# An interaction tower (DLRM): layer blocks moved between gram and lookups, and the copies shared out anew

## The chip, the cores and the metric

One core of one Trainium2 chip. The metric is the device time of one launch in microseconds, the median of several runs. Times inside a run are from the profile, in us from the start of its span.

## The reference

2048 samples, 27 features. Each feature is a row of 128 floats from a table of its own (1000 to 125000 rows). All pairs of the 27 rows of a sample are multiplied (351 products), and three layers follow.

```python
e = jnp.stack([tbl_0[ids[:, 0]], ..., tbl_26[ids[:, 26]]], axis=1)
x = einsum('bfd,bgd->bfg', e, e)[pairs with g < f]
z = concatenate([bottom, x], axis=1)
h = concatenate([z, bottom], axis=1)
h = maximum(h @ W_top1 + b_top1, 0.0)
h = maximum(h @ W_top2 + b_top2, 0.0)
y = h @ W_top3
```

W_top1 is 607x512, W_top2 512x256, W_top3 256x1. All is fp32.

## The kernel before

The samples go through in 16 halves of 128 (`HALF`). Two halves make a tile of 256, and the layers work on units (`u`): seven whole tiles and the last tile in two units of 128.

Features come in two ways. 17 tables are **gathered**: GpSimd (POOL) issues one indirect DMA for each table and half (L311), into `rows`, a ring of two halves; five groups of 4, 4, 3, 3 and 3 tables. TensorE turns each group (`transpose`, L705, three or four transposes into a column bank) and ScalarE or VectorE copies it into `eT`. Ten small tables are **looked up** (hot tables): VectorE compares ids with row numbers to make 0/1 masks (`make_masks`, L582 and L586), and TensorE multiplies table parts by the masks (`look_up`, L686). One lookup serves a window of four halves, so each half has one or two lookups (32 or 52 matmul records x2) for later halves. Their results are copied from the column banks to `eH` (L424 on ScalarE, L599 on VectorE) and placed in `eT` by ScalarE (`place_hot`, L438). There are three column banks, used in the order of the list `FILLS`; `on_scalar` tells which engine copies a fill.

`multiply_pairs` (the gram, L722) multiplies the features of each sample with each other; ScalarE and VectorE copy the result into `pairs` (`copy_pairs`, L468 and L617), and SyncE moves it into `x` in nine DMAs (`load_x`). The last half's nine are shared by SyncE, ScalarE and GpSimd.

The layers: `layer1(u, blocks)` has four blocks m = 0 to 3, each of 4 matmuls (one with `bottom` at L741, three with `x` at L745; fp32 matmuls show as two records each, so a block has 8). `layer2` (L777) has 8 matmuls, `layer3` (L787) 8 small ones. Blocks 0 and 1 and layer 2 write `mlp_bank[0]`, blocks 2 and 3 and layer 3 `mlp_bank[1]`. ScalarE does `relu1` (L477), `relu2` (L484) and `copy_y` (L493). For the last unit `last_layer1_bottom` (L756) and `last_layer1_pairs` (L766) use the free column and gram banks.

Each engine runs its own list written out by hand; semaphores tie them together. TensorE's for a half h, before:

```python
for g in groups_of(h): transpose(h, g)
if h % 2 == 0:
    layer3(h // 2 - 2); layer1(h // 2 - 1, range(2))
elif h >= 3: layer2(h // 2 - 1)
multiply_pairs(h)
for n in AFTER[h]: look_up(n)
if h % 2 == 0: layer1(h // 2 - 1, range(2, 4))
```

GpSimd's list has only the gathers, each group waiting until the group two halves earlier is transposed, then the last three DMAs of x.

Of the kernel before, what the change touches and what calls it, by code (L numbers as in the profile page):

```python
# [133 lines left out]
def on_scalar(fill):  # L134

    return fill < FRONT_FILLS or fill % 2 == 1
# [9 lines left out]
def build(nc, tables, idx_d, hot_ids_d, bottom_d, w1_d, wa_d, wb_d, b1_d, w2_d, b2_d, w3_d, ident_d, rowid_d, out_d):  # L146
# [6 lines left out]
    with ctx:  # L153
# [133 lines left out]
        def layer3_out(u):  # L287
            _, _, size = unit_columns(u)
            if u == TILES:
                return gram_bank[0].rearrange("p q g -> p (q g)")[:, 0:size // Y_STRIPS]  # L290
            return mlp_bank[1][:, 0, 0:size // Y_STRIPS]
# [41 lines left out]
        def _(sp):  # L333
# [62 lines left out]
            for h in range(HALVES):  # L396
                if h % 2 == 0:
                    load_bottom(h // 2)
                    if h >= 4:
                        store_y(h // 2 - 2)  # L400
# [4 lines left out]
            store_y(TILES - 2)  # L405
            store_y(TILES - 1)
# [4 lines left out]
        def _(act):  # L411
# [59 lines left out]
            def relu1(u, b):  # L471
                _, at, size = unit_columns(u)
                act.wait_ge(l1_full, 2 * u + b + 1)
# [51 lines left out]
            for h in range(1, HALVES):  # L525
                for g in groups_of(h):
                    copy_transposed(h, g)
                if h % 2 == 0 and h >= 4:
                    copy_y(h // 2 - 2)
                copy_pairs(h)  # L530
                if h % 2 == 0:
                    relu1(h // 2 - 1, 0)
                elif h >= 3:
                    relu2(h // 2 - 1)
# [9 lines left out]
            for r in range(1, len(BLOCKS), 3):  # L544
                out, src = x_block(LAST, r)
                nc.scalar.dma_start(out, src).then_inc(x_loaded[LAST % 2], 16)
            copy_y(TILES - 2)
            relu1(TILES - 1, 0)
            relu1(TILES - 1, 1)
# [10 lines left out]
        def _(dve):  # L560
# [30 lines left out]
            def copy_lookup(n):  # L591
                for k in LOOKUPS[n][0]:
                    fill = lookup_fill(n, k)
                    if not on_scalar(fill):

                        dve.wait_ge(col_full[fill % BANKS], fill // BANKS + 1)
                        dve.wait_ge(hot_copied, LOOKUPS[n][1])
                        out, src = looked_up(n, k)
                        nc.vector.tensor_copy(out, src).then_inc(col_copied[fill % BANKS], 1)  # L599

# [36 lines left out]
            def masks_behind_gram(h):  # L637

                n = AFTER[h][0]
                pair_used = entries_to(n + 1) + MASKS  # L640
                make_entries(entries_to(n) + MASKS, pair_used)
                copy_lookup(n)
                for single in AFTER[h][1:]:
                    make_entries(pair_used, entries_to(single + 1) + MASKS)
                    copy_lookup(single)
# [18 lines left out]
        def _(pe):  # L664
# [63 lines left out]
            def layer1(u, blocks):  # L728
                buf, at, size = unit_columns(u)
                for m in blocks:  # L730
                    if m == 0:
# [4 lines left out]
                        if u > 0:  # L736
                            pe.wait_ge(h2_made, u)
# [147 lines left out]
```

## Time and profile before

| what | value |
|---|---|
| median of 3 runs | 411.26 us (410.33 to 411.98) |
| the profiled execution | 408.87 us, span 406.9 us |
| TensorE matmul busy | 355.6 us, 87% |
| GpSimd busy | 293.9 us, 72% |
| VectorE busy | 231.5 us, 57% |
| ScalarE busy | 156.5 us, 38% |
| mean granted clock of TensorE | 0.966 of full |

The span runs from the first to the last instruction; the execution's own time is 2 us longer. Busy time of GpSimd counts the gather instructions alone, the 0.30 us between them are not in it.

### The profile page before, as it was taken

To read this page: it belongs to the slowest core of one execution; us is meant where nothing else is said; L and a number is where in the kernel's file an instruction comes from. 1 tells how busy PE (TensorE), PEld (TensorE's weight loads), DVE (VectorE), ACT (ScalarE), POOL (GpSimd) and SP (SyncE) were. 2 spreads that over 40 slices of the span, in tenths; PEclk is the share of its full clock that TensorE was granted. 3 is DMA by queue.
4 is the path that set the end of the run, shared out by engine and by line. 5 is a ranking of instruction groups with operands and counts; after the bars stand their busy time and mean duration, and the time that the engine had idled before them with its cause. 6 is when DMAs were issued, how large, how long until landed. Compare 5 with 4: busy or idle time off the path is not lost.

```text
span 406.9 us, 9147 instructions
## 1 busy us (share of the span) xinstructions
PE 355.6 (87%) x3669; PEld 305.4 (75%) x3669; DVE 231.5 (57%) x430; ACT 156.5 (38%) x337; POOL 293.9 (72%) x284
## 2 busy tenths in 40 slices
PE   0679888979997999989996999989997899869986
PEld 0678667858885888868885788868885798749876
DVE  1588985857747274858746173856746163816120
ACT  2245624225343244325352243425244153505342
POOL 5777887777777787777777777777778777777210
PEclk9999996999999899999999799999999899969999
DMA  7968952323414131323324222322513222322100
GB/s 194 249 183 218 269 149 69 116 78 82 149 53 129 55 86 57 117 72 109 126 58 124 54 73 67 115 79 78 144 53 100 57 74 65 85 72 68 32 21 2
DMA packets 20737, 40.50 MB, mean 100 GB/s; under 512 B 7128, under 2 KB 11428, under 8 KB 20696
## 3 DMA queue, kind: packets, MB, share of 16 engines
q1 hardware_dynamic: 11674, 21.64, 18.6%
q0 software_dynamic: 8960, 18.22, 16.5%
q8 instruction: 29, 0.48, 0.5%
q14 instruction: 12, 0.10, 0.1%
q10 hardware_dynamic: 62, 0.06, 0.1%
HBM read 36.81 MB, written 0.01 MB: 90 GB/s over the span
## 4 chain that ended last, share of the span: by engine, by line
PE 48%; POOL 33%; issue 11%; DMA 4%; DVE 2%; DVEq 1%; ACT 0%; ACTq 0%
POOL rows L311 31%; PE col_bank L686 17%; PE gram_bank L722 9%; PE mlp_bank L745 9%; PE col_bank L705 4%; PE mlp_bank L777 4%; DMA rows<-in_tbl,idx 4%; PE mlp_bank L741 3%; POOL h L322 1%; DVEq L589 1%; PE mlp_bank L787 1%; DVE mask L582 1%; DVE mask L586 1%; DMA idx<-in_gather_ids 1%; PE gram_bank L777 1%
## 5 line engine op out<-in xcount | busy, mean ns | idle before, releaser
L311 POOL DMA_INDIRECT rows<-in_tbl,idx x272 | 286.4, 1053 | 85.4 <-issue 79.5
L686 PE MATMUL col_bank<-mask,parts 125*128 125x512 f32 (+3 forms) x768 | 163.7, 374 | 16.5 <-DVE mask L582 16.5
L686 PEld LDWEIGHTS col_bank<-mask,parts 125*128 125x128 f32 x768 | 135.8, 198 | 39.0 <-DVE parts L623 15.6
L582 DVE TENSOR_SCALAR mask<-hot_i,rowid 125x1024 fp32r<-125x1024 int32 (+3 forms) x152 | 103.4, 681 | 20.0 <-PE col_bank L686 9.8
L617 DVE COPY pairs<-gram_bank 26x208 f32<-26x208 f32 x128 | 46.7, 365 | 79.4 <-PE gram_bank L722 58.0
L468 ACT ACTIVATE pairs<-gram_bank 26x208 f32<-26x208 f32 x128 | 44.3, 346 | 80.1 <-PE gram_bank L722 60.4
L705 PE MATMUL col_bank<-ident,rows 128*128 128x128 f32 x272 | 41.3, 290 | 27.4 <-DMA rows<-in_tbl,idx 14.3
L722 PEld LDWEIGHTS gram_bank<-eT 128*58 128x58 f32 x2048 | 56.9, 135 | 7.9 <-issue 7.6
L722 PE MATMUL gram_bank<-eT 128*58 128x52 f32 x2048 | 59.0, 218 | 2.4 <-ACT eT L438 1.6
L705 PEld LDWEIGHTS col_bank<-ident,rows 128*128 128x128 f32 x272 | 31.8, 147 | 36.2 <-DMA rows<-in_tbl,idx 17.1
L438 ACT ACTIVATE eT<-eH 128x256 f32<-128x256 f32 (+1 forms) x64 | 43.4, 790 | 17.8 <-DVE eH L599 16.9
L424 ACT ACTIVATE eH<-col_bank 128x512 f32<-128x512 f32 (+3 forms) x30 | 15.2, 516 | 87.5 <-PE col_bank L686 77.1
L745 PE MATMUL mlp_bank<-x,w 126*128 126x256 f32 (+3 forms) x192 | 48.4, 391 | 0.0
L607 DVE COPY eT<-col_bank 128x384 f32<-128x384 f32 (+2 forms) x42 | 25.3, 611 | 38.3 <-PE col_bank L705 37.5
L745 PEld LDWEIGHTS mlp_bank<-x,w 126*128 126x128 f32 (+1 forms) x192 | 38.1, 207 | 6.2
L586 DVE TENSOR_SCALAR mask<-hot_i,rowid 125x512 fp32r<-125x512 int32 (+2 forms) x80 | 33.6, 467 | 5.0 <-PE col_bank L686 1.9
L432 ACT ACTIVATE eT<-col_bank 128x384 f32<-128x384 f32 (+2 forms) x41 | 21.7, 553 | 19.4 <-PE col_bank L705 19.2
L777 PE MATMUL mlp_bank<-h,w 128*128 128x256 f32 (+1 forms) x128 | 27.4, 367 | 0.0
L777 PEld LDWEIGHTS mlp_bank<-h,w 128*128 128x128 f32 x128 | 22.6, 190 | 2.5
L741 PE MATMUL mlp_bank<-bottom,w 128*128 128x256 f32 (+1 forms) x64 | 21.2, 416 | 0.0
L623 DVE TENSOR_TENSOR parts<-pairs,parts 125x1024 fp32r<-125x1024 f32 (+1 forms) x10 | 12.6, 1281 | 12.1 <-ACT parts L415 6.1
L477 ACT ACTIVATE h<-mlp_bank,b 128x256 f32<-128x256 f32 (+1 forms) x32 | 13.0, 457 | 13.5 <-PE mlp_bank L745 13.2
(34 smaller groups left out, 75.6 us busy)
## 6 DMA issues: line engine op xcount, KB each, us to landing
hot_i<-in_hot_ids SPq DMA_DIRECT2D x13, 512.0 KB, 4.0
rows<-in_tbl,idx POOLq DMA_INDIRECT x272, 3.0
pairs<-in_tbl SPq DMA_DIRECT2D x8, 448.0 KB
hot_i<-in_hot_ids SPq DMA_DIRECT2D x8, 256.0 KB, 3.3
pairs<-in_tbl SPq DMA_DIRECT2D x2, 560.0 KB
bottom<-in_bottom SPq DMA_DIRECT2D x8, 128.0 KB, 4.0
hot_i<-in_hot_ids SPq DMA_DIRECT2D x2, 384.0 KB, 4.6
x<-pairs SPq DMA_DIRECT2D x16, 39.0 KB
```

What stands on the lines that cost most here:

```text
L311: pool.indirect_dma_start(out=rows_of(h, g)[:, i * D:(i + 1) * D], out_offset=None, in_=tables[GATHERED_TABLES[f]], in_offset=bass.Indirec ...
L438: return nc.scalar.activation(eT[:, :, first:last].rearrange("p s f -> p f s"), eH[:, first:last, at:at + HALF], ACT.Copy)
L468: last = nc.scalar.activation(pairs_of(s, 1, j), gram_of(n % BANKS, 1, j), ACT.Copy)
L582: last = nc.vector.tensor_scalar(mask[0:ROWS, entry % MASKS, 0:2 * size], ids, row_of(ks[0], c), None, ALU.is_equal)
L586: last = nc.vector.tensor_scalar(mask[0:ROWS, entry % MASKS, i * size:(i + 1) * size], ids, row_of(ks[0], 2 * c + i), None, ALU.is_equal)
L617: last = nc.vector.tensor_copy(pairs_of(s, 0, j), gram_of(n % BANKS, 0, j))
L686: last = nc.tensor.matmul(col_bank[fill % BANKS][:, 0:size], parts[k][0:ROWS, part, c * D:(c + 1) * D], mask[0:ROWS, entry % MASKS, at:at ...
L705: last = nc.tensor.transpose(col_bank[fill % BANKS][:, i * HALF:(i + 1) * HALF], src, ident[:, :])
L722: last = nc.tensor.matmul(gram_bank[n % BANKS][COLUMNS * t:COLUMNS * t + GRAM_ROWS, q, 0:PACK * (F - 1)], eT[:, a:a + PACK, :].rearrange(" ...
L741: nc.tensor.matmul(layer1_out(u, m), w1[:, X_CHUNKS, m * 128:(m + 1) * 128], bottom[:, buf, at:at + size], start=True, stop=False)
L745: last = nc.tensor.matmul(layer1_out(u, m).rearrange("p (h s) -> p h s", s=HALF), w1[0:k, c, m * 128:(m + 1) * 128], x[0:k, buf, at // HAL ...
L777: last = nc.tensor.matmul(layer2_out(u, m), w2[:, c, m * 128:(m + 1) * 128], h1[:, c, at:at + size], start=(c == 0), stop=(c == N1 // 128 ...
```

## The change

- `on_scalar`: ScalarE copies every lookup; of the five groups of transposes in a half it copies 1 and 3 (from half 1 on), VectorE 0, 2 and 4 (and the extra group 5 goes to ScalarE). Before, odd fills went to ScalarE and even ones to VectorE, whatever they were.
- VectorE: `copy_lookup` is gone, and `masks_behind_gram` makes the same masks in the same order in one go.
- TensorE: layer 1's blocks run in the order 2, 3, 0, 1. Block 2 stands ahead of an even half's gram, blocks 3 and 0 behind its lookups, block 1 ahead of the odd half's gram, and layer 2 behind that half's lookups. Layer 3 moves from the even half to the odd one behind it.
- The tail: behind the last transposes stand layer 3 of unit 5, block 1 of unit 6, the gram, layer 2 of unit 6, the bottom matmuls of the last unit, layer 1 of unit 7, layer 3 of unit 6 (now in a gram bank), layer 2 of unit 7; from there it is as before.
- ScalarE and SyncE follow: `relu2` in even halves, `copy_y` and `relu1(u, 0)` in odd ones ahead of `copy_pairs`; the store of y one even half later; in the tail ScalarE issues its three DMAs of x ahead of `relu2` of unit 6.

TensorE's rows around the last two halves' transposes, before: from the transposes of half 14 (L705, from `rows` into `col_bank`) over layer 3 (L787) and layer 1 (L741, L745) to the gram (L722), the lookups (L686), two blocks and the transposes of half 15.

```order
L705 MATMUL col_bank<-ident,rows 128x128 x17
L787 MATMUL mlp_bank<-h,w 32x64 x8
L741 MATMUL mlp_bank<-bottom,w 128x256
L745 MATMUL mlp_bank<-x,w 128x256 x3
L741 MATMUL mlp_bank<-bottom,w 128x256
L745 MATMUL mlp_bank<-x,w 128x256 x3
L722 MATMUL gram_bank<-eT 58x52 x64
L686 MATMUL col_bank<-mask,parts 128x128 x52
L741 MATMUL mlp_bank<-bottom,w 128x256
...
L705 MATMUL col_bank<-ident,rows 128x128 x17
```

The same place in the changed kernel (its lines are L692 for transposes, L728 and L732 for layer 1, L709 for the gram, L673 for lookups, L781 for layer 3):

```order
L692 MATMUL col_bank<-ident,rows 128x128 x17
L728 MATMUL mlp_bank<-bottom,w 128x256
L732 MATMUL mlp_bank<-x,w 128x256 x3
L709 MATMUL gram_bank<-eT 58x52 x64
L673 MATMUL col_bank<-mask,parts 128x128 x52
L728 MATMUL mlp_bank<-bottom,w 128x256
...
L692 MATMUL col_bank<-ident,rows 128x128 x17
L781 MATMUL mlp_bank<-h,w 32x64 x8
L728 MATMUL mlp_bank<-bottom,w 128x256
L732 MATMUL mlp_bank<-x,w 128x256 x3
L709 MATMUL gram_bank<-eT 58x52 x64
```

One block and layer 3 have moved from between the two halves' transposes to behind the last ones. What stood behind the last transposes before, up to layer 2 of unit 7:

```order
L777 MATMUL mlp_bank<-h,w 128x256 x8
L722 MATMUL gram_bank<-eT 58x52 x64
L787 MATMUL mlp_bank<-h,w 32x64 x8
L741 MATMUL mlp_bank<-bottom,w 128x128
...
L756 MATMUL col_bank<-bottom,w 128x128 x3
L756 MATMUL gram_bank<-bottom,w 128x128
L777 MATMUL mlp_bank<-h,w 128x128 x8
```

And now, from layer 2 of unit 6 on (L765 is layer 2, L744 the bottom matmuls):

```order
L765 MATMUL mlp_bank<-h,w 128x256 x8
L744 MATMUL col_bank<-bottom,w 128x128 x3
L744 MATMUL gram_bank<-bottom,w 128x128
L728 MATMUL mlp_bank<-bottom,w 128x128
...
L781 MATMUL gram_bank<-h,w 32x64 x8
L765 MATMUL mlp_bank<-h,w 128x128 x8
```

Layer 2 of unit 6 stands behind the gram instead of ahead of it, and the bottom matmuls ahead of layer 1 of unit 7 instead of behind it.

```diff
--- before.py
+++ after.py
@@ -133,7 +133,8 @@
 
 def on_scalar(fill):
 
-    return fill < FRONT_FILLS or fill % 2 == 1
+    what = FILLS[fill]
+    return fill < FRONT_FILLS or what[0] == "lookup" or what[2] % 2 == 1
 
 
 def unit_columns(u):
@@ -286,8 +287,9 @@
 
         def layer3_out(u):
             _, _, size = unit_columns(u)
-            if u == TILES:
-                return gram_bank[0].rearrange("p q g -> p (q g)")[:, 0:size // Y_STRIPS]
+            if u in (TILES - 2, TILES):
+                first = 0 if u < TILES else TILE // Y_STRIPS
+                return gram_bank[0].rearrange("p q g -> p (q g)")[:, first:first + size // Y_STRIPS]
             return mlp_bank[1][:, 0, 0:size // Y_STRIPS]
 
         block = ctx.enter_context(nc.Block())
@@ -396,14 +398,14 @@
             for h in range(HALVES):
                 if h % 2 == 0:
                     load_bottom(h // 2)
-                    if h >= 4:
-                        store_y(h // 2 - 2)
+                    if h >= 6:
+                        store_y(h // 2 - 3)
                 load_x(h, range(0, len(BLOCKS), 3) if h == LAST else range(len(BLOCKS)))
                 if h + 1 < LAST:
                     for n in AFTER[h + 1][1:] + (AFTER[h + 2][:1] if h + 2 < LAST else []):
                         load_hot_ids(n)
-            store_y(TILES - 2)
-            store_y(TILES - 1)
+            for t in range(TILES - 3, TILES):
+                store_y(t)
 
             sp.wait_ge(y_stored, 16 * TILES)
 
@@ -470,7 +472,7 @@
 
             def relu1(u, b):
                 _, at, size = unit_columns(u)
-                act.wait_ge(l1_full, 2 * u + b + 1)
+                act.wait_ge(l1_full, 2 * u + (1 if b == 1 else 2))
                 if u == 0 and b == 0:
                     act.wait_ge(w1_summed, 1)
                 for m in range(2 * b, 2 * b + 2):
@@ -526,12 +528,12 @@
                 for g in groups_of(h):
                     copy_transposed(h, g)
                 if h % 2 == 0 and h >= 4:
-                    copy_y(h // 2 - 2)
+                    relu2(h // 2 - 2)
+                elif h >= 3:
+                    if h >= 5:
+                        copy_y(h // 2 - 2)
+                    relu1(h // 2 - 1, 0)
                 copy_pairs(h)
-                if h % 2 == 0:
-                    relu1(h // 2 - 1, 0)
-                elif h >= 3:
-                    relu2(h // 2 - 1)
                 if h < LAST:
                     place_early(h + 1)
                     for n in AFTER[h]:
@@ -544,9 +546,10 @@
             for r in range(1, len(BLOCKS), 3):
                 out, src = x_block(LAST, r)
                 nc.scalar.dma_start(out, src).then_inc(x_loaded[LAST % 2], 16)
+            relu2(TILES - 2)
+            relu1(TILES - 1, 1)
+            relu1(TILES - 1, 0)
             copy_y(TILES - 2)
-            relu1(TILES - 1, 0)
-            relu1(TILES - 1, 1)
             relu2(TILES - 1)
             for m in range(N1 // 128):
                 act.wait_ge(l1_full, 2 * TILES + m + 1)
@@ -588,16 +591,6 @@
                     last.then_inc(masks_made, 1)
                     dve.drain()
 
-            def copy_lookup(n):
-                for k in LOOKUPS[n][0]:
-                    fill = lookup_fill(n, k)
-                    if not on_scalar(fill):
-
-                        dve.wait_ge(col_full[fill % BANKS], fill // BANKS + 1)
-                        dve.wait_ge(hot_copied, LOOKUPS[n][1])
-                        out, src = looked_up(n, k)
-                        nc.vector.tensor_copy(out, src).then_inc(col_copied[fill % BANKS], 1)
-
             def copy_transposed(h, g):
                 fill = transpose_fill(h, g)
                 if not on_scalar(fill):
@@ -636,13 +629,7 @@
 
             def masks_behind_gram(h):
 
-                n = AFTER[h][0]
-                pair_used = entries_to(n + 1) + MASKS
-                make_entries(entries_to(n) + MASKS, pair_used)
-                copy_lookup(n)
-                for single in AFTER[h][1:]:
-                    make_entries(pair_used, entries_to(single + 1) + MASKS)
-                    copy_lookup(single)
+                make_entries(entries_to(AFTER[h][0]) + MASKS, entries_to(AFTER[h][-1] + 1) + MASKS)
 
             for k in LATE:
                 make_low(k)
@@ -728,16 +715,16 @@
             def layer1(u, blocks):
                 buf, at, size = unit_columns(u)
                 for m in blocks:
-                    if m == 0:
+                    if m == 2:
 
                         for half in ((0, 1) if u < TILES - 1 else (0,)):
                             pe.wait_ge(x_loaded[half], 16 * len(BLOCKS) * (u + 1))
                         pe.wait_ge(bottom_loaded[buf], 16 * (u // 2 + 1))
-                        if u > 0:
-                            pe.wait_ge(h2_made, u)
-                    if m == 2 and u > 0:
-
-                        pe.wait_ge(y_made, u)
+                        if u > 1:
+                            pe.wait_ge(y_made, u - 1)
+                    if m == 0 and u > 0:
+
+                        pe.wait_ge(h2_made, u)
                     nc.tensor.matmul(layer1_out(u, m), w1[:, X_CHUNKS, m * 128:(m + 1) * 128], bottom[:, buf, at:at + size],
                                      start=True, stop=False)
                     for c in range(X_CHUNKS):
@@ -752,6 +739,7 @@
             def last_layer1_bottom():
 
                 pe.wait_ge(gram_copied[1], STRIPS * used(HALVES * SETS, 1))
+                pe.wait_ge(bottom_loaded[(TILES - 1) % 2], 16 * ((TILES - 1) // 2 + 1))
                 for m in range(N1 // 128):
                     nc.tensor.matmul(layer1_out(TILES, m), w1[:, X_CHUNKS, m * 128:(m + 1) * 128],
                                      bottom[:, (TILES - 1) % 2, HALF:TILE], start=True, stop=False)
@@ -781,6 +769,12 @@
             def layer3(u):
                 _, at, size = unit_columns(u)
                 pe.wait_ge(h2_made, u + 1)
+                if u < TILES - 2:
+
+                    pe.wait_ge(h1_made, 2 * (u + 1) + 1)
+                elif u == TILES - 2:
+
+                    pe.wait_ge(gram_copied[0], STRIPS * used(HALVES * SETS, 0))
                 part = size // Y_STRIPS
                 for c in range(N2 // 128):
                     for t in range(Y_STRIPS):
@@ -804,26 +798,30 @@
                 for g in groups_of(h):
                     transpose(h, g)
                 if h % 2 == 0:
-                    if h >= 4:
-                        layer3(h // 2 - 2)
                     if h == 2:
                         pe.wait_ge(weights_loaded, 16 * WEIGHT_LOADS)
                         pe.wait_ge(w1_summed, 1)
-                    layer1(h // 2 - 1, range(2))
+                    layer1(h // 2 - 1, (2,))
                 elif h >= 3:
-                    layer2(h // 2 - 1)
+                    if h >= 5:
+                        layer3(h // 2 - 2)
+                    layer1(h // 2 - 1, (1,))
                 multiply_pairs(h)
                 for n in AFTER[h]:
                     look_up(n)
                 if h % 2 == 0:
-                    layer1(h // 2 - 1, range(2, 4))
+                    layer1(h // 2 - 1, (3, 0))
+                elif h >= 3:
+                    layer2(h // 2 - 1)
             for g in range(NG):
                 transpose(LAST, g)
+            layer3(TILES - 3)
+            layer1(TILES - 2, (1,))
+            multiply_pairs(LAST)
             layer2(TILES - 2)
-            multiply_pairs(LAST)
+            last_layer1_bottom()
+            layer1(TILES - 1, (2, 3, 0, 1))
             layer3(TILES - 2)
-            layer1(TILES - 1, range(4))
-            last_layer1_bottom()
             layer2(TILES - 1)
             last_layer1_pairs()
             layer2(TILES)
```

## Rows read from the trace of the kernel before

**Rows 1.** Page, busy us (share of the span) x instructions.
```profile
PE 355.6 (87%) x3669; PEld 305.4 (75%) x3669; DVE 231.5 (57%) x430; ACT 156.5 (38%) x337; POOL 293.9 (72%) x284
```

**Rows 2.** Page, groups: count | busy us, mean ns | idle before, releaser.
```profile
L311 POOL DMA_INDIRECT rows<-in_tbl,idx x272 | 286.4, 1053 | 85.4 <-issue 79.5
```

**Rows 3.** Waits of POOL: us in total, times, longest us.
```profile
POOL rows L311 <- PE col_bank L705: 1.8, 6, 0.3
```

**Rows 4.** Timeline of POOL, its last gather: start us, us, instruction.
```profile
378.58 0.94 POOL L311 DMA_INDIRECT rows<-in_tbl,idx  x1 [0.30 <-issue]
```

**Rows 5.** Waits of PE, the two largest behind the start.
```profile
PE col_bank L705 <- DMA rows<-in_tbl,idx: 14.3, 10, 3.6
PE col_bank L705 <- DVE eH L599: 7.4, 5, 3.1
```

**Rows 6.** Timeline of PE, 300 to 407 us.
```profile
356.21 0.52 PE L705 MATMUL col_bank<-ident,rows 128*128 128x128 f32 x3 [1.47 <-DMA rows<-in_tbl,idx]
360.29 0.90 PE L705 MATMUL col_bank<-ident,rows 128*128 128x128 f32 x3 [3.56 <-DMA rows<-in_tbl,idx]
...
361.71 1.22 PE L741 MATMUL mlp_bank<-bottom,w 128*128 128x256 f32 x2
362.72 2.75 PE L745 MATMUL mlp_bank<-x,w 124*128 124x256 f32 x6
...
376.54 0.65 PE L741 MATMUL mlp_bank<-bottom,w 128*128 128x256 f32 x2
...
380.06 2.35 PE L705 MATMUL col_bank<-ident,rows 128*128 128x128 f32 x17
382.25 3.62 PE L777 MATMUL mlp_bank<-h,w 128*128 128x256 f32 x16
385.80 3.62 PE L722 MATMUL gram_bank<-eT 128*58 128x52 f32 x128
391.07 0.43 PE L787 MATMUL mlp_bank<-h,w 128*32 128x64 f32 x16 [1.65 <-ACT h L484]
391.43 0.49 PE L741 MATMUL mlp_bank<-bottom,w 128*128 128x128 f32 x2
...
395.35 0.83 PE L756 MATMUL col_bank<-bottom,w 128*128 128x128 f32 x6
...
396.24 2.04 PE L777 MATMUL mlp_bank<-h,w 128*128 128x128 f32 x16
```

**Rows 7.** Chain that ended last; then the gathers' tile, 350 to 385.
```profile
357.35 2.90 DMA rows<-in_tbl,idx
...
DMA to landing us min/median/max: 2.4/2.6/3.5
```

**Rows 8.** Timeline of all engines, 194.9 to 196.5 us.
```profile
195.01 0.94 POOL L311 DMA_INDIRECT rows<-in_tbl,idx  x1 [0.30 <-issue]
195.12 0.69 DVE L599 COPY eH<-col_bank 128x512 f32<-128x512 f32 x1 [0.16 <-issue]
...
196.26 1.18 POOL L311 DMA_INDIRECT rows<-in_tbl,idx  x1 [0.30 <-issue]
```

**Rows 9.** Windows: PE, PEld, DVE, ACT, POOL busy, PEclk, DMA, GB/s.
```profile
128.00:220.00 92.00, 85.92 (x880) 72.29 (x878) 55.17 (x102) 35.54 (x78) 71.58 (x68) 0.98 0.30 90
220.00:311.00 91.00, 85.74 (x869) 71.85 (x870) 52.16 (x97) 35.08 (x77) 70.58 (x68) 0.96 0.30 87
```

**Rows 10.** Timeline of all engines, 376 to 407 us.
```profile
391.47 1.61 ACTq L546 DMA_DIRECT2D x<-pairs  x2
...
395.55 0.62 ACT L477 ACTIVATE h<-mlp_bank,b 128x128 f32<-128x128 f32 x2 [1.40 <-PE mlp_bank L745]
```

**Rows 11.** Timeline of PE, 0 to 200 us.
```profile
62.36 3.01 PE L705 MATMUL col_bank<-ident,rows 128*128 128x128 f32 x13 [3.13 <-DVE eH L599]
...
177.57 0.84 PE L705 MATMUL col_bank<-ident,rows 128*128 128x128 f32 x6 [1.80 <-DVE eT L607]
```

**Rows 12.** Windows of PE: us, busy (count), PEclk, DMA share, GB/s.
```profile
364.00:365.00 1.00, 1.00 (x4) 0.50 0.19 62
```

## The prediction

> **What bounds the kernel now.** I read the busy shares first, then GpSimd's stream, then what TensorE waits for, and last the end of the run in order of time. TensorE is busy 87% of the span [rows 1], which looks like the bound. It isn't the one that sets the pace. GpSimd's group of gathers shows 272 gathers of 1.053 us each and 85.4 us idle, 79.5 of it only issue [rows 2]: 0.30 us ahead of each gather, as the two of [rows 8] show. Its longest wait put down to TensorE is also 0.3 us [rows 3], so it never waited for a transpose to free a buffer. It starts its last gather at 378.58 and ends it at 379.52 [rows 4]. TensorE on the other hand waits for landed rows 10 times, 14.3 us in all [rows 5]. The worst is at half 14: it transposes three tables at 356.21, then stands 3.56 us until the last group has landed and goes on at 360.29 [rows 6]; the chain shows that transfer as the releaser, 2.90 us after its issue [rows 7]. So up to half 14 the gathers set the time, and TensorE catches up with them again and again. From 360.29 it has 19.8 us of work up to the last half's transposes at 380.06 [rows 6], and the last gathers land just then. In this one stretch TensorE and GpSimd are level; everything behind 382.25 is a tail of TensorE alone.
>
> **The change part by part.** The sum is made on the profiled execution, 408.87 us with a span of 406.9; the median of the runs shown is 411.26, 2.4 more, and I add my difference to that.
>
> *Layer 1 and 2 in the halves.* No matmul is added or removed. A unit's work was 4 blocks of layer 1 and the 2 blocks of layer 2, and an even half carried all four layer 1 blocks, one of 1.76 us (two take 376.54 to 380.06 [rows 6]), an odd half layer 2, 3.55 us (382.25 to 385.80). Now an even half has three layer 1 blocks and an odd one layer 3 (0.36, 391.07 to 391.43), the fourth block and layer 2. TensorE comes 2.1 us later to the transposes of even halves, where it waits for rows anyway, and 2.1 us sooner to those of odd halves, the last half's among them, since block m=1 and layer 3 are no longer ahead of them. What it finds there is rows that haven't landed. Price in the halves: 0, covered by GpSimd's stream, which doesn't wait for TensorE; if that cover were gone, these microseconds would be a gain.
>
> *Two blocks between lookups and transposes.* Before, the transposes of an even half came right behind the lookups and waited for copies out of the column banks: 7.4 us in 5 waits for VectorE's lookup copies [rows 5]. These go, with 3.5 us of layer work in front of them. Late next are the landed rows; so 0 again.
>
> *Who copies.* VectorE gives up its 16 lookup copies and ScalarE takes them, one or so in each half, at about the 0.69 us that VectorE needs [rows 8]. ScalarE then places the hot columns, then copies its two groups of transposes. Its queue grows by 0.7 us a half, where 3.5 us of matmuls now give it room. In half 2 there is no layer work behind half 1's lookups; a stall of a microsecond is possible there, and the wait for rows at half 4 covers it. VectorE copies three of five groups in every half. For GpSimd the question is whether its gathers get quicker. They take 0.94 us in quiet and more beside masks: 1.18 at 196.26 beside the mask instructions. Beside a lookup copy (195.12, 0.69 us) the gather of 195.01 takes 0.94 [rows 8]. All masks stay, so their price of 272 x (1.053 - 0.94) = 31 us stays. It could drift with the phase of masks against gathers: two stretches of four halves with the same masks have 71.58 and 70.58 us of GpSimd for 68 gathers [rows 9]. From this I take 0 and, over the whole run, 1 us either way. The bounds without this argument are the full 31 us below, excluded since no mask is dropped, and a like amount above, excluded since no mask is added.
>
> *SyncE.* The store of y moves one even half later, and the loads of x stay in place; a store stands behind nothing that TensorE waits for until the tail, where the y of unit 6 is needed only for the last layer 3 copy, some 6 us later. 0.
>
> *The tail.* The last transposes can't start before the last three gathers have landed. The last one is issued at 378.58; landing took 2.4 to 3.5 us, median 2.6, in this stretch [rows 7]. With 2.6 they land at 381.2, and three transposes take 0.5 (356.21), which gives 381.7 against the 382.25 of before (there the copy of a bank was also late): -0.55, between -0.75 and +0.4.
> Behind them stood before: layer 2 3.55, gram 3.62 with a wait of 1.65 for ScalarE's h2, layer 3 0.36, layer 1 of unit 7 3.92 (391.43 to 395.35), the bottom blocks 0.89, and layer 2 of unit 7 at 396.24: 13.99 us [rows 6].
> Now stand there: layer 3 of unit 5 0.36, layer 1's block m=1 1.76, gram 3.6, layer 2 3.55, bottom 0.89, layer 1 of unit 7 3.92, and then a wait. The bottom blocks used to cover ScalarE's relu (395.55, 0.62 us [rows 10]); now only layer 3's 0.36 lies there, so from the end of layer 1 to layer 2 it stays 0.89. Sum 14.97, that is +0.98. The wait of 1.65 is gone, and in its place stand the block of 1.76 and layer 3's 0.36 that came in from half 14, and the bare relu.
> The relu of layer 2 of unit 6 is now queued on ScalarE behind its three transfers of x, two of which took 1.61 us [rows 10]; with gram ending 3 to 4 us before layer 2 does, it runs near the end of layer 2, and layer 1 needs it only after two blocks and the bottom (about 2.8 us). 0. Everything behind 396.24 is unchanged.
> Total: -0.55 + 0.98 = +0.4 us. The forecast is 411.7, its own range 410.4 to 413.1 (1 us of GpSimd's drift and the bounds of the landing).
>
> **The rivals.** Within 0.5%, 2.06 us, a measurement of this kernel can't tell from no change.
>
> *B, slower: TensorE's clock is low in the tail.* TensorE now waits longer in one piece. A wait of 1.80 us at 177 left the matmuls at full speed; one of 3.13 us ahead of 62.36 was followed by 13 transposes in 3.01 us [rows 11], against 0.52 for three (356.21). After the waits of 356 to 360 the granted clock was 0.50, 1.2 GHz, still in 364 to 365 [rows 12], and a block took from 361.71 to 365.47, 3.7 us, against 1.8. Whether this happens at the last transposes hangs on half 14. If the clock is low there as before, TensorE comes to the last transposes 1.76 and some 0.5 sooner than 380.06, near 377.8, needs 1.8 for the first 14 and waits 1.6 us until 381.2: no fall. If half 14 runs at full speed, it is there 2.2 sooner, near 375.6, and waits over 3 us: a fall. In half 14 TensorE was free at 354.74 (356.21 less the wait of 1.47 [rows 6]); 2.1 later and with three more transposes that is 357.3, a wait of 3.0 before 360.29, at the edge as well. So it could go either way. The price is transposes 0.4 and the block 1.9, 2.2 with rounding: 411.7 + 2.2 = 413.9. It decides once the wait before the last three transposes is beyond about 3 us.
> The Trainium skill (TensorE: Matmul & The Clock Gate, section "Why this matters for your kernels") warns against idle gaps between bursts, since the array goes back to half rate. It speaks against this change, which puts TensorE's waits together; by that rule alone B would be the forecast. The trace agrees for 3.13 us and not for 1.80.
>
> *A, faster: gathers gain from VectorE's missing copies.* If a lookup copy cost GpSimd what a mask does, 1.18 - 0.94 = 0.24 us, 16 fewer would give 4 us: 407.7. Against it stands the gather of 0.94 beside the copy [rows 8].
> The Trainium skill (SBUF — State Buffer, section "Who interferes with whom") counts copies among VectorE's operations that can take the port pair shared with GpSimd. Measured by its word alone A would hold; the row here speaks against it for a copy out of PSUM.
>
> *C, faster: TensorE is the bound after all.* Then the vanished stalls count: 7.4 us for lookup copies, and with them 411.3 - 7.4 = 403.9. It needs GpSimd to be waiting somewhere, and [rows 2, 3] show no such place.
>
> **How the numbers follow.** The forecast has 54%: 3 of them over 0.5% faster, 5 slower by the drift, 46 in between. B has 32%: 27 slower, 5 still within 0.5%, since 413.3 is the border. A has 10%, C 4%, both faster. That makes faster 0.17, same 0.51, slower 0.32. The range takes in the forecast and B with their bounds, from 409.4 to 414.4, and leaves A and C out.
>
> **What would show it.** In the changed profile GpSimd's gathers still run without a pause and end near 379.5; TensorE's waits for lookup copies are nearly gone and its waits for landed rows are up from 14.3 to over 20 us; the last transposes end near 381.7; layer 2 of unit 7 starts near 396.7, at full clock. If it starts near 399 with a granted clock of 0.50 behind the last transposes, B is right. If the last gather ends before 377, A is. If gathers show pauses above 0.3 us, my bound is wrong.

## The result, and the profile after

The changed kernel takes 413.15 us, the median of 15 runs (411.8 to 414.15); the kernel before took 410.82 us beside it (15 runs, 408.74 to 412.85). The ratio is 1.0047 with a 95% interval of 1.003 to 1.0064: slower by 1.9 us, 0.5%, at the very border of what counts as no change here. The interval reaches from 1.2 to 2.6 us, and the two medians as they stand are 2.3 us apart. The change's profiled execution took 413.02 us with a span of 411.2, near its median. The profiled execution of before, at 408.87, was 2 us below its own. So the two spans, 411.2 and 406.9, lie 4.3 us apart, of which about half belongs to these two samples and not to the change.

From the page of the changed kernel, first the busy times, then GpSimd's group:

```profile
PE 356.6 (87%) x3669; PEld 305.4 (74%) x3669; DVE 223.9 (54%) x417; ACT 162.9 (40%) x350; POOL 296.7 (72%) x284
...
L313 POOL DMA_INDIRECT rows<-in_tbl,idx x272 | 287.9, 1059 | 85.3 <-issue 79.9
```

As before [rows 1, 2]: TensorE 87% busy, and GpSimd's 272 gathers at 1.059 us, with 79.9 of the 85.3 us ahead of them only issue and no wait for TensorE above 0.3 us. TensorE's waits in the changed kernel (us in total, times, longest us):

```profile
PE col_bank L692 <- DMA rows<-in_tbl,idx: 25.9, 14, 3.3
...
PE col_bank L692 <- DVE eT L600: 3.8, 2, 2.9
...
PE mlp_bank L765 <- ACT h L479: 0.4, 1, 0.4
```

The 7.4 us for lookup copies [rows 5] are gone. The waits for landed rows have grown from 14.3 to 25.9 us. That is most of the story of the halves: what TensorE no longer waits for copies, it waits for rows.

The tail in TensorE's timeline (start us, us, instruction, idle before and its releaser); it answers to [rows 6], from the last half's transposes to layer 2 of unit 7:

```profile
379.00 2.00 PE L692 MATMUL col_bank<-ident,rows 128*128 128x128 f32 x14
383.81 0.85 PE L692 MATMUL col_bank<-ident,rows 128*128 128x128 f32 x3 [2.82 <-DMA rows<-in_tbl,idx]
384.59 0.65 PE L781 MATMUL mlp_bank<-h,w 128*32 128x64 f32 x16
385.17 1.22 PE L728 MATMUL mlp_bank<-bottom,w 128*128 128x256 f32 x2
386.18 2.03 PE L732 MATMUL mlp_bank<-x,w 124*128 124x256 f32 x6
388.14 3.62 PE L709 MATMUL gram_bank<-eT 128*58 128x52 f32 x128
...
400.59 2.05 PE L765 MATMUL mlp_bank<-h,w 128*128 128x128 f32 x16 [0.35 <-ACT h L479]
```

and the granted clock behind the wait (us, busy, clock, DMA share, GB/s):

```profile
384.00:385.00 1.00, 1.00 (x19) 0.50 0.00 0
...
386.00:387.00 1.00, 1.00 (x3) 0.50 0.00 0
387.00:388.00 1.00, 1.00 (x5) 0.84 0.00 0
```

TensorE is done with 14 of 17 transposes at 381.0, stands 2.82 us, and comes back at 0.50 of the clock, 1.2 GHz. Layer 3 then takes 0.58 instead of 0.36 and the block 2.97 from 385.17 to 388.14, where half 14's own block at full clock takes 1.83 (364.24 to 366.07). That is rival B of the prediction. From the start of the last gather to layer 2 of unit 7 it is 19.36 us (381.23 to 400.59) against 17.66 before (378.58 to 396.24): the tail has 1.7 of the 4.3 us between the spans.

### The profile page after: what moved, and what is told of

It reads as the page before. It is cut to its first block, busy times and chain, and to the rows that moved or that the text cites. A ratio compares the mean times of both kernels' runs of the same rounds, so it can differ in the third digit from the quotient of the medians.

```text
span 411.2 us, 9138 instructions
## 1 busy us (share of the span) xinstructions
PE 356.6 (87%) x3669; PEld 305.4 (74%) x3669; DVE 223.9 (54%) x417; ACT 162.9 (40%) x350; POOL 296.7 (72%) x284
## 4 chain that ended last, share of the span: by engine, by line
POOL 37%; PE 32%; issue 13%; DMA 9%; DVE 5%; DVEq 2%; ACT 1%; SPq 1%; POOLq 0%
POOL rows L313 37%; PE col_bank L673 11%; PE gram_bank L709 7%; PE mlp_bank L732 4%; DVE mask L585 4%; DMA rows<-in_tbl,idx 4%; PE mlp_bank L765 3%; DMA hot_i<-in_hot_ids 3%; PE col_bank L692 2%; DVEq L592 2%; PE mlp_bank L728 2%; DMA pairs<-in_tbl 2%; DMA h<-in_tbl,idx 1%; PE gram_bank L765 1%; ACT parts L417 0%
## 5 line engine op out<-in xcount | busy, mean ns | idle before, releaser
L313 POOL DMA_INDIRECT rows<-in_tbl,idx x272 | 287.9, 1059 | 85.3 <-issue 79.9
L673 PE MATMUL col_bank<-mask,parts 125*128 125x512 f32 (+3 forms) x768 | 162.8, 372 | 17.3 <-DVE mask L585 17.3
L673 PEld LDWEIGHTS col_bank<-mask,parts 125*128 125x128 f32 x768 | 134.8, 197 | 39.9 <-DVE parts L616 15.7
L600 DVE COPY eT<-col_bank 128x384 f32<-128x384 f32 (+1 forms) x45 | 27.5, 616 | 76.4 <-PE col_bank L692 75.3
L692 PE MATMUL col_bank<-ident,rows 128*128 128x128 f32 x272 | 40.4, 286 | 30.8 <-DMA rows<-in_tbl,idx 25.9
L709 PEld LDWEIGHTS gram_bank<-eT 128*58 128x58 f32 x2048 | 58.3, 137 | 9.4 <-issue 9.4
L709 PE MATMUL gram_bank<-eT 128*58 128x52 f32 x2048 | 60.3, 221 | 2.7 <-ACT eT L440 2.1
L426 ACT ACTIVATE eH<-col_bank 128x512 f32<-128x512 f32 (+3 forms) x46 | 22.5, 530 | 96.1 <-PE col_bank L673 95.9
L692 PEld LDWEIGHTS col_bank<-ident,rows 128*128 128x128 f32 x272 | 31.2, 144 | 39.2 <-DMA rows<-in_tbl,idx 30.1
L732 PE MATMUL mlp_bank<-x,w 126*128 126x256 f32 (+3 forms) x192 | 50.0, 400 | 0.0
L732 PEld LDWEIGHTS mlp_bank<-x,w 126*128 126x128 f32 (+1 forms) x192 | 38.9, 211 | 6.4
L434 ACT ACTIVATE eT<-col_bank 128x384 f32<-128x384 f32 (+3 forms) x38 | 20.2, 545 | 43.3 <-PE col_bank L692 43.3
L765 PE MATMUL mlp_bank<-h,w 128*128 128x256 f32 (+1 forms) x128 | 27.5, 367 | 0.4 <-ACT h L479 0.4
L765 PEld LDWEIGHTS mlp_bank<-h,w 128*128 128x128 f32 x128 | 22.9, 190 | 3.5 <-ACT h L479 0.5
L728 PE MATMUL mlp_bank<-bottom,w 128*128 128x256 f32 (+1 forms) x64 | 21.3, 417 | 0.0
```

The lines of the kernel that those rows point to most:

```text
L313: pool.indirect_dma_start(out=rows_of(h, g)[:, i * D:(i + 1) * D], out_offset=None, in_=tables[GATHERED_TABLES[f]], in_offset=bass.Indirec ...
L673: last = nc.tensor.matmul(col_bank[fill % BANKS][:, 0:size], parts[k][0:ROWS, part, c * D:(c + 1) * D], mask[0:ROWS, entry % MASKS, at:at ...
L692: last = nc.tensor.transpose(col_bank[fill % BANKS][:, i * HALF:(i + 1) * HALF], src, ident[:, :])
L709: last = nc.tensor.matmul(gram_bank[n % BANKS][COLUMNS * t:COLUMNS * t + GRAM_ROWS, q, 0:PACK * (F - 1)], eT[:, a:a + PACK, :].rearrange(" ...
L728: nc.tensor.matmul(layer1_out(u, m), w1[:, X_CHUNKS, m * 128:(m + 1) * 128], bottom[:, buf, at:at + size], start=True, stop=False)
L732: last = nc.tensor.matmul(layer1_out(u, m).rearrange("p (h s) -> p h s", s=HALF), w1[0:k, c, m * 128:(m + 1) * 128], x[0:k, buf, at // HAL ...
```

## Where the rest of the span's difference came from

GpSimd's last gather starts later than in [rows 4]:

```profile
381.23 0.95 POOL L313 DMA_INDIRECT rows<-in_tbl,idx  x1 [0.30 <-issue]
```

That is 2.65 us behind 378.58. Its timeline in the changed kernel at the start, with its 21st and its 34th gather last:

```profile
10.99 1.89 POOL L313 DMA_INDIRECT rows<-in_tbl,idx  x1 [0.30 <-issue]
...
20.96 1.92 POOL L313 DMA_INDIRECT rows<-in_tbl,idx  x1 [0.30 <-issue]
...
28.19 1.96 POOL L324 DMA_INDIRECT h<-in_tbl,idx  x1 [0.31 <-issue]
...
31.71 1.13 POOL L313 DMA_INDIRECT rows<-in_tbl,idx  x1 [0.30 <-issue]
...
51.00 0.95 POOL L313 DMA_INDIRECT rows<-in_tbl,idx  x1 [0.30 <-issue]
```

and in the kernel before, the same two last:

```profile
7.22 1.95 POOL L311 DMA_INDIRECT rows<-in_tbl,idx  x1 [0.30 <-issue]
...
28.20 1.97 POOL L311 DMA_INDIRECT rows<-in_tbl,idx  x1 [0.30 <-issue]
30.47 0.96 POOL L311 DMA_INDIRECT rows<-in_tbl,idx  x1 [0.30 <-issue]
...
49.78 0.94 POOL L311 DMA_INDIRECT rows<-in_tbl,idx  x1 [0.31 <-issue]
```

Single gathers take 1.9 us in the first 30 us of both, three of them in one trace and two in the other. By the 21st gather the changed kernel is 1.24 us behind (31.71 against 30.47), by the 34th 1.22. The rest comes later: from the 34th gather to the last it is 328.80 us before and 330.23 after, 1.4 us more, most of it from gathers beside masks, which take 1.0 to 1.6 us. So about half of the 2.65 us is from the start and half is drift. Whether that drift comes of the moved copies or would show between two traces of one kernel, a single full trace of before can't say.

## The experiments

The theory after the result: the change is slower because its tail starts with a long wait and then runs at half the clock. The rival: GpSimd's gathers end later because masks and copies now meet them differently. All kernels with a label ending in b or c are repeats, since on three of the chips used every kernel, the one before too, took over 530 us. What those chips did is told further down.

**One block in the wait (e5b).** The changed kernel with one block of layer 1 computed twice.

```diff
-            for g in range(NG):
+            for g in range(NG - 1):
                 transpose(LAST, g)
+            layer1(TILES - 2, (0,))
+            transpose(LAST, NG - 1)
             layer3(TILES - 3)
             layer1(TILES - 2, (1,))
```

> Once more on another chip, since on the first one every kernel took over 530 us. The changed kernel with one block of layer 1 (unit 6, m=0, the same values once more) computed a second time ahead of the last group of transposes. Clock theory: the wait there shrinks from about 3 us to 1.3, the clock stays at its full level, and the time falls by 2.2 us to about 0.4 above before, although TensorE does more. Rival (gathers end later since the copies moved): 2 us slower than before.

Measured: 410.8 us (12 runs) against 410.65 of before, ratio 1.0006 (0.9989 to 1.0023). TensorE computes 4 more matmuls and the time is 1.7 us less than the change's (1.0047 less 1.0006, of 411). The two weren't measured side by side but each against before; from the two intervals I estimate the 1.7 as good to 1 us either way. Its timeline of TensorE, then the last gather, then the clock:

```profile
377.62 2.00 PE L692 MATMUL col_bank<-ident,rows 128*128 128x128 f32 x14
379.46 0.60 PE L728 MATMUL mlp_bank<-bottom,w 128*128 128x256 f32 x2
...
382.53 0.55 PE L692 MATMUL col_bank<-ident,rows 128*128 128x128 f32 x3 [1.18 <-DMA rows<-in_tbl,idx]
383.01 0.43 PE L781 MATMUL mlp_bank<-h,w 128*32 128x64 f32 x16
383.37 0.70 PE L728 MATMUL mlp_bank<-bottom,w 128*128 128x256 f32 x2
...
385.30 3.62 PE L709 MATMUL gram_bank<-eT 128*58 128x52 f32 x128
...
397.75 2.05 PE L765 MATMUL mlp_bank<-h,w 128*128 128x128 f32 x16 [0.35 <-ACT h L479]
```

```profile
379.80 0.94 POOL L313 DMA_INDIRECT rows<-in_tbl,idx  x1 [0.30 <-issue]
```

```profile
383.00:384.00 1.00, 1.00 (x20) 1.00 0.00 0
```

The wait is 1.18 us instead of 2.82, and the clock stays at 1.00. From the last transposes to layer 2 of unit 7 it is 15.22 us (382.53 to 397.75) against 16.78 in the change (383.81 to 400.59): 1.56 us, which is the 1.7 of the medians. The work between the two points is the same. The clock theory holds. The late gathers can't explain this: they end 1.4 us earlier in this one trace, but with that taken out, from the last gather to layer 2 of unit 7, it is still 17.95 us (379.80 to 397.75) against 19.36, and medians of 12 and 15 runs hang little on one trace's gathers.

**Only the copies (e1b).** The kernel before with the new `on_scalar`, VectorE's `copy_lookup` taken out and its masks made in one go.

```diff
-    return fill < FRONT_FILLS or fill % 2 == 1
+    what = FILLS[fill]
+    return fill < FRONT_FILLS or what[0] == "lookup" or what[2] % 2 == 1
...
```

> Once more on another chip. The kernel before with the copies alone changed. Clock theory: no difference, within 0.5 us of before, since the tail is that of before. Rival (gathers): about 2 us slower than before, and the last gather starts near 381 instead of 378.6.

Measured: 411.76 us against 410.65, ratio 1.0025 (1.0002 to 1.0047), between the two expectations. GpSimd's timeline, the 34th gather and the last, and TensorE's tail:

```profile
51.06 0.94 POOL L312 DMA_INDIRECT rows<-in_tbl,idx  x1 [0.30 <-issue]
...
381.14 0.94 POOL L312 DMA_INDIRECT rows<-in_tbl,idx  x1 [0.30 <-issue]
```

```profile
384.11 3.62 PE L762 MATMUL mlp_bank<-h,w 128*128 128x256 f32 x16
...
398.14 2.04 PE L762 MATMUL mlp_bank<-h,w 128*128 128x128 f32 x16
```

The last gather is as late as in the change, at 381.14: 1.28 us behind before by the 34th gather, and another 1.28 from there to the last (330.08 us against 328.80). The tail from layer 2 of unit 6 to that of unit 7 is 14.03 us against 13.99 in [rows 6], so the copies cost nothing there. In e5b, which has the same copies, the stretch from the 34th gather to the last is 329.20 us, 0.4 more than before, and the time is level with before, at most 0.9 us above it by its interval. So the three traces with moved copies drift by 0.4, 1.3 and 1.4 us against the one of before. What the copies have in that, and in the 1.0 us of this run, whose interval reaches down to 0.1 us, is left open.

**Fewer gathers (f1, f2).** Both kernels without the gathers of the last two tables from half 2 on, 28 of 277; their products are made of stale rows.

```diff
                         f = first + i
+                        if h >= 2 and f >= GATHERED - 2:
+                            continue
```

> The kernel before without the gathers of the last two tables from half 2 on: 28 of 277 are left out, and stale rows stand in their place in the products. If GpSimd's stream paces the kernel, 28 x 1.36 = 38 us less of it moves the bound to TensorE: the time falls by about the waits for rows (14 us) and the time at half clock behind them (some 6), to about 391, and no further. If TensorE is the bound already, it stays within 2 us of before.

> The changed kernel without the same 28 gathers. Pace theory: here the waits for copies that the change removed count at last, so it is faster than the kernel before with fewer gathers by 5 to 9 us, about 384. Rival (the change gains nothing on TensorE either): equal to or slower than the other by the 2 us that it loses now.

Measured: before with fewer gathers 387.81 us (ratio 0.9421 to before, 0.9351 to 0.9492), the change with fewer 375.77 (0.915, 0.9098 to 0.9202). The bound was GpSimd's stream: without a tenth of it both get faster. And the change, worth -1.9 us as it stands, is worth 12.0 us by the medians of 4 runs each (11 by the two ratios) once GpSimd is out of the way, where I expected 5 to 9. The kernel before fell further than the 391 that I expected too: TensorE's busy time went down from 355.6 to 345.7 us at the same number of matmuls, its mean granted clock up from 0.966 to 0.990. In the changed kernel it went from 356.6 to 344.3 us and from 0.963 to 0.995. From these busy times I estimate that the matmuls at half clock cost TensorE 10 to 12 us in the full kernels, not some 6. TensorE's waits in the kernel before with fewer gathers, and the one that GpSimd now has for TensorE:

```profile
PE col_bank L707 <- DVE eH L601: 7.5, 5, 3.1
PE col_bank L707 <- DVE eT L609: 5.0, 3, 1.8
PE col_bank L707 <- ACT eT L434: 2.8, 4, 0.9
...
PE mlp_bank L789 <- ACT h L486: 1.7, 1, 1.7
```

```profile
POOL rows L313 <- PE gram_bank L724: 7.6, 3, 4.0
```

and in the changed one:

```profile
PE col_bank L694 <- DVE eT L602: 3.7, 2, 2.9
...
PE col_bank L694 <- DMA rows<-in_tbl,idx: 1.6, 3, 0.6
```

These four are 17.0 us of waits for copies (7.5, 5.0, 2.8, 1.7) on one side, against 3.7 with 1.6 for rows on the other. All of TensorE's waits together are 36.5 us against 25.6, 10.9 of the 11.6 us between the two spans (385.1 and 373.5). GpSimd, never held up for more than 0.3 us in the full kernel, waits for the gram here, 7.6 us. So rival C had the gain right in kind, and it can't be collected as long as the 277 gathers run until 379.5 us.

**The wait filled with work that is due (e3).** In the last half, layer 3 of unit 5 and block m=1 of unit 6 go ahead of the last group, and a block of unit 7 covers the copy ahead of the gram.

```diff
-            for g in range(NG):
+            for g in range(NG - 1):
                 transpose(LAST, g)
             layer3(TILES - 3)
             layer1(TILES - 2, (1,))
+            transpose(LAST, NG - 1)
+            layer1(TILES - 1, (2,))
             multiply_pairs(LAST)
...
-            layer1(TILES - 1, (2, 3, 0, 1))
+            layer1(TILES - 1, (3, 0, 1))
```

> A third time, since both chips of the first two took over 530 us for every kernel. The changed kernel, but in the last half layer 3 of unit 5 and block m=1 of unit 6 stand ahead of the last group of transposes, and block m=2 of unit 7 between it and the gram. Clock theory: about 3.1 us after the last gather starts the transposes are done, then 0.98 + 3.6 + 3.55 + 0.89 + 2.94 + 0.89 = 12.9, so 16.0 us to layer 2 of unit 7: 1.7 us faster than before. Rival (the end is set elsewhere, by the transfers of x or ScalarE's queue): layer work put into the wait comes back as a later wait, and the time is that of before.

This was run three times and came to a slow chip each time: 547.1 us against 557.1, 548.25 against 549.19 (ratio 0.9946, 0.9872 to 1.0019), 563.09 against 569.53. It was the lower each time, but the runs of both spread over 11 to 33 us, and the one interval there is includes an equal time. What the trace does show is the tail's own length:

```profile
530.04 1.99 PE L692 MATMUL col_bank<-ident,rows 128*128 128x128 f32 x14
...
534.16 0.49 PE L692 MATMUL col_bank<-ident,rows 128*128 128x128 f32 x3
534.49 0.39 PE L728 MATMUL mlp_bank<-bottom,w 128*128 128x128 f32 x2
...
535.48 3.62 PE L709 MATMUL gram_bank<-eT 128*58 128x52 f32 x128
...
547.04 2.05 PE L765 MATMUL mlp_bank<-h,w 128*128 128x128 f32 x16 [0.35 <-ACT h L479]
```

From the last group's transposes at 534.16 to layer 2 of unit 7 at 547.04 it is 12.88 us with no new wait in it, against 15.22 in e5b and 16.78 in the change, which have more of the layers behind those transposes. Behind the transposes themselves it is 12.55 us (534.49 to 547.04), where I expected 12.9. There the rows had long landed, so how much of it would show on an undisturbed chip, 1.7 us below before by my sum, isn't measured.

**The runs on the slow chips.** Layers alone, the second profile of before, and the first tries of the above say nothing about 2 us. What was expected of the first four, on one chip:

> The kernel before with the copies alone changed: ScalarE copies all lookups, VectorE three of five groups and its masks in one go; the layers stay where they were. Clock theory (the change is slower because its tail begins with a long wait and runs at half the clock): no difference, within 0.5 us of before, since the tail is that of before. Rival (GpSimd's gathers end later because the masks and copies hit them differently): about 2 us slower than before, and the last gather starts near 381 instead of 378.6.

> The changed kernel with the copies of before: odd fills on ScalarE, even ones on VectorE, lookups among them. Clock theory: like the change, 2 us slower than before, with about 3 us of wait ahead of the last three transposes and a granted clock of 0.50 behind them. Rival (gathers): no slower than before, within 0.5 us.

> The changed kernel, but in the last half layer 3 of unit 5 and block m=1 of unit 6 stand ahead of the last group of transposes, and block m=2 of unit 7 between it and the gram. Clock theory: the 2.1 us of layer work go into the wait, the clock stays high, and from landing at 381.2 the steps 0.5 + 0.98 + 3.6 + 3.55 + 0.89 + 2.94 + 0.89 put layer 2 of unit 7 at 394.6 instead of 396.2: 1.7 us faster than before, 4 us faster than the change. Rival (gathers): only the 2.1 us of moved work, so as fast as before.

> The changed kernel with one block of layer 1 (unit 6, m=0, the same values once more) computed a second time ahead of the last group of transposes: eight more matmul records in the wait and nothing else. Clock theory: the wait shrinks from about 3 us to 1.3, the clock stays at its full level, and the time falls by 2.2 us to about 0.4 above before, although TensorE does more. Rival (gathers): no change, 2 us slower than before; a block that isn't fully covered would add to that.

They took 553.25, 555.72, 547.1 and 550.81 us, with 557.1 for before, whose own executions lay between 536.58 and 564.05. On the second such chip the filled wait took 548.25 us, 549.19 being before:

> Once more on another chip. The changed kernel, but in the last half layer 3 of unit 5 and block m=1 of unit 6 stand ahead of the last group of transposes, and block m=2 of unit 7 between it and the gram. Clock theory, now with 17.7 us from the start of the last gather to layer 2 of unit 7 before and 19.4 in the change: here about 3.1 us after the last gather starts the transposes are done, then 0.98 + 3.6 + 3.55 + 0.89 + 2.94 + 0.89 = 12.9, so 16.0 us: 1.7 us faster than before. Rival (the end is set elsewhere, by the transfers of x or ScalarE's queue): layer work put into the wait comes back as a later wait, and the time is that of before.

The layers alone once more on that chip:

> Once more on another chip. The changed kernel with the copies of before. Clock theory: like the change, 2 us slower than before. If the copies have a share of their own (copies alone gave 1.0 us, 0.1 to 1.9), this one is only 1 us slower.

552.74 us against 549.19 of before, whose executions lay between 538.68 and 571.78. The layers alone stay unmeasured, and with them the share of the copies. And the second profile of before:

> The kernel before, unchanged, for a second profile of it. If the later start of the last gather in the change (381.2 against 378.6) is chance in the first 30 us and not the change, this one has its last gather anywhere from 378.5 to 381.5, and 276 us between the first gathers of half 3 and half 15 as all others have. If it is the change, this one starts its last gather at 378.6 again.

570.37 us, useless for the purpose. That gathers start late by chance rests on the traces of the undisturbed chips. Up to half 2 f1 is the kernel before and f2 the changed one, and there it is the changed one that is ahead: the 21st gather starts at 30.47 in before and 30.83 in f1, at 31.71 in the change and 30.34 in f2 (31.77 in e1b, 31.32 in e5b). For the drift behind it there is no second trace of before.

## Why the prediction was right, and where its sum was off

The forecast was no change, 411.7 us in a range of 409.4 to 414.4; measured 413.15, ratio 1.0047. The time is in the range, on the border of 0.5%, and it lies between my forecast (+0.4) and my rival B (+2.6). By mechanism it was B, to which I gave 32%, and not the forecast. That no change came out all the same is luck: B cost 1.6 to 1.7 us and not 2.2, and the ratio stayed just inside 0.5%.

- *The gathers set the pace, so the vanished waits of TensorE are worth 0.* Right. 14.3 us of waits for rows became 25.9, and f1 and f2 show the other side.
- *Moved copies and masks leave the gathers as they are.* Not shown either way. The gathers still run without a pause, but from the 34th to the last they take 0.4, 1.3 and 1.4 us more in the three traces with moved copies than in the one of before. The medians leave room for 1 us (e1b) or less (e5b).
- *The drift of 1 us either way.* The kind was right, the size too small for a single execution: 1.4 us, and on top of it 1.2 us that the sum didn't have, from gathers of 1.9 us in the first 30 us.
- *The tail, -0.55 + 0.98.* The full-clock tail is in e5b: the last transposes end 3.21 us after the last gather starts (379.80 to 383.01), where I had 2.6 and 0.5, and then it is 14.74 us to layer 2 of unit 7, where I summed 14.97; and +0.2 us in the medians for my +0.4. The wait for the bare relu is there (0.4 us in 1 wait), as is the end of the old one for h2.
- *The step that failed: "if the clock is low there as before, ... no fall", taken for likelier.* Half 14 ran at full speed in the changed kernel, TensorE was at the last transposes at 379.00, 2.2 us before the last gather started, and stood 2.82 us. I had set the point of decision beyond about 3 us; here 2.82 was enough. Why half 14 was fast, the sum had nothing on: the odd halves now wait for rows too, and half 13 had the long wait and the low clock, so TensorE came late to half 14 and waited only 1.51 us there, where I had 3.0. From its last three transposes over layer 3 and the block to the gram, half 13 took 5.13 us (341.11 to 346.24); the same work at full clock is 2.77 us in e5b (382.53 to 385.30). Some waits of the changed kernel, half 13's at 341.11 and half 14's at 363.86 among them, with what followed:

```profile
156.31 0.55 PE L692 MATMUL col_bank<-ident,rows 128*128 128x128 f32 x3 [2.19 <-DMA rows<-in_tbl,idx]
...
249.71 0.55 PE L692 MATMUL col_bank<-ident,rows 128*128 128x128 f32 x3 [2.89 <-DMA rows<-in_tbl,idx]
...
250.55 1.02 PE L728 MATMUL mlp_bank<-bottom,w 128*128 128x256 f32 x2
251.37 2.77 PE L732 MATMUL mlp_bank<-x,w 124*128 124x256 f32 x6
...
341.11 0.90 PE L692 MATMUL col_bank<-ident,rows 128*128 128x128 f32 x3 [3.06 <-DMA rows<-in_tbl,idx]
...
342.53 1.22 PE L728 MATMUL mlp_bank<-bottom,w 128*128 128x256 f32 x2
...
363.86 0.55 PE L692 MATMUL col_bank<-ident,rows 128*128 128x128 f32 x3 [1.51 <-DMA rows<-in_tbl,idx]
```

A wait of 2.19 us is followed by matmuls at full speed, one of 2.89 us by a block of 1.02 and 2.77, half speed. The length of the last wait alone doesn't settle it: in e5b one of 2.72 us ahead of 318.46 left the block behind it at full speed (1.83 us, 318.84 to 320.67), while in the kernel before waits of 2.12 and 1.19 us, ahead of 315.38 and 317.11 with three transposes between them, were followed by a granted clock of 0.50. The Trainium skill's warning (TensorE: Matmul & The Clock Gate, section "Why this matters for your kernels") against idle gaps between bursts was the better guide. The waits of 2.82, 2.89 and 3.06 us agree with it; those of 1.51, 2.19 and 2.72 us are gaps that cost no clock.
- *B's price, 2.2 us.* It is 1.6 in the trace and 1.7 in the medians: against e5b the transposes lost 0.3, layer 3 0.2 and the block 1.0, not 1.9, since the clock came back within it (0.84 in 387 to 388).
- *Rival A.* Excluded: VectorE has 16 lookup copies fewer, and the last gather starts 1.2 to 2.65 us later than before in all three full traces, not 4 us earlier.

## What to carry to other kernels

Before taking waits off the busiest engine, look whether a less busy one runs without a pause: its stream is the bound, and what you save turns into a longer wait elsewhere. A longer wait in one piece isn't always free on TensorE: here one of 2.82 us was followed by a granted clock of 0.50, and the tail behind it took 1.6 us longer. A redundant block in the wait brought that back; putting work in that is due should do better by my sum, which no run on an undisturbed chip shows. And when a change fails for such a reason, leave the bound out in an experiment: it tells what the change is worth later, here 11 to 12 us.

## What was not expected of the hardware

In the first 30 us of GpSimd's stream single gathers took 1.5 to 2.0 us instead of 0.94, twice or three times in each of the six traces of undisturbed chips, and not always the same ones. Since the stream sets the pace, each can shift the end by up to 1 us.

On three chips every kernel took 534 to 575 us. The waits in the profile of the kernel before on one of them (us in total, times, longest us):

```profile
POOL rows L311 <- PE gram_bank L722: 144.9, 14, 27.6
...
PEld gram_bank L722 <- issue: 69.3, 79, 1.9
...
PE gram_bank L722 <- issue: 52.9, 70, 1.8
```

TensorE's gram, 128 small matmul records that take 3.6 us elsewhere, is broken by dozens of waits of about 0.7 us put down to issue, and GpSimd then waits for the gram, 144.9 us in all. What slows the issue there, the profile doesn't say. All seven other kernels profiled on these chips show the same two waits, 109 us or more for the gram on GpSimd and 60 us or more of issue at the gram.
